# Row maxima of 64-row halves of the array, and key rows interleaved by four, in an attention and expert kernel

## The reference

```python
def _L0_xattn_ref(x, context, w_qkv, w_proj, b_proj):
    B, N, C = x.shape                      # 8, 256, 128
    H, D = 16, 8
    qkv = (x @ w_qkv.T).reshape(B, N, 3, H, D).transpose(2, 0, 3, 1, 4)
    q, k, v = (qkv[0], qkv[1], qkv[2])
    kv = context.reshape(B, N_c, 2, H, D).transpose(2, 0, 3, 1, 4)
    k = jnp.concatenate([kv[0], k], axis=2)
    v = jnp.concatenate([kv[1], v], axis=2)
    attn = jnp.einsum('bhnd,bhmd->bhnm', q * D ** -0.5, k).astype(jnp.float32)
    attn = jax.nn.softmax(attn, axis=-1)
    out = jnp.einsum('bhnm,bhmd->bhnd', attn, v)
    return out.transpose(0, 2, 1, 3).reshape(B, N, C) @ w_proj.T + b_proj

x = x + _L0_xattn_ref(_layernorm(x), ctx_2048, ...)
x = x + _L0_ffn_ref(_layernorm(x), ...)    # experts; the change leaves this part alone
```

## Time and profile before

| | |
|---|---|
| median of 3 runs | 580.87 us (580.58 to 586.15) |
| the profiled execution: its own time | 579.1 us |
| its span, first to last instruction | 577.5 us |
| attention | about 0 to 370 us |
| router and experts | about 370 to 577 us |
| PE busy over the span | 498.9 us (86%) |
| DVE, ACT, POOL busy | 353.9, 292.7, 196.0 us |

### The profile page before, as it was taken

One profiled execution on the slowest core, in us unless ns is written; L12 is line 12 of the kernel. 1 busy time (PEld: TensorE's weight loads), 2 busy tenths in 40 slices (PEclk: granted clock), 3 DMA queues, 4 the chain that ended last, 5 costly groups with the idle time before them and its releaser, 6 DMA issues. The chain is left out here.

```text
span 577.5 us, 10586 instructions
## 1 busy us (share of the span) xinstructions
PE 498.9 (86%) x3467; PEld 322.9 (56%) x3468; DVE 353.9 (61%) x646; ACT 292.7 (51%) x584; POOL 196.0 (34%) x381
## 2 busy tenths in 40 slices
PE   3479999999999999999999998555499999999940
PEld 1346666666666666666565663244447666666630
DVE  7597687777777787777777770368524333333316
ACT  2136667767767677676776767421023333333310
POOL 7151241331422412411400000103317776677630
PEclk9999999999999999999999999865569999999995
DMA  6802434445244344342332300160101111111116
GB/s 168 185 25 72 94 88 108 95 105 134 75 113 121 87 120 104 91 115 64 76 72 58 90 3 2 36 184 0 14 10 43 41 41 38 39 36 43 42 51 189
DMA packets 32078, 44.39 MB, mean 77 GB/s; under 512 B 5484, under 2 KB 20460, under 8 KB 32036
## 3 DMA queue, kind: packets, MB, share of 16 engines
q1 hardware_dynamic: 27076, 36.88, 25.7%
q0 software_dynamic: 2560, 5.25, 3.6%
q10 hardware_dynamic: 2400, 1.70, 1.2%
HBM read 16.58 MB, written 4.72 MB: 37 GB/s over the span
## 5 line engine op out<-in xcount | busy, mean ns | idle before, releaser
L426 DVE TENSOR_REDUCE max_part<-max_ps 128x2 f32<-128x1024 f32 (+1 forms) x192 | 231.3, 1221 | 79.6 <-PE max_ps L519 42.1
L385 ACT ACTIVATE probs<-exp_ps 128x512 f32<-128x512 f32 x384 | 207.4, 591 | 77.5 <-PE exp_ps L541 72.0
L541 PE MATMUL exp_ps<-blocks,keys 128*128 128x512 f32 x384 | 160.9, 421 | 4.5 <-ACT probs L385 2.3
L519 PE MATMUL max_ps<-keys,blocks 128*128 128x512 f32 x256 | 109.9, 436 | 10.1 <-DMA blocks<-masked 7.0
L541 PEld LDWEIGHTS exp_ps<-blocks,keys 128*128 128x128 f32 x384 | 71.7, 187 | 44.8 <-ACT probs L385 18.5
L551 PE MATMUL pv_ps<-probs,value_cols 128*32 128x256 f32 x1536 | 96.3, 383 | 0.0
L986 DVE TENSOR_TENSOR hidden<-up_ps,silu 128x512 f32<-128x512 f32 x40 | 27.7, 692 | 84.4 <-PE up_ps L1076 82.4
L302 POOL CAST maxes<-rowmax 128x8 fp32r<-128x8 f32 x32 | 6.3, 198 | 178.6 <-DVE rowmax L432 178.6
L519 PEld LDWEIGHTS max_ps<-keys,blocks 128*128 128x128 f32 x256 | 48.4, 191 | 30.2 <-DVE max_part L426 19.2
L551 PEld LDWEIGHTS pv_ps<-probs,value_cols 128*32 128x32 f32 x1536 | 43.3, 109 | 39.4 <-issue 17.1
L879 ACT ACTIVATE hiddenT<-at_ps 128x512 f32<-128x512 f32 x40 | 23.9, 597 | 77.2 <-PE at_ps L1093 68.7
(11 more groups left out here) (148 smaller groups left out, 473.4 us busy)
## 6 DMA issues: line engine op xcount, KB each, us to landing
blocks<-masked SPq DMA_DIRECT2D x93, 128.0 KB
keys<-parts SPq DMA_DIRECT2D x96, 96.0 KB
ctx_v_sb<-ctx_v_dram SPq DMA_DIRECT2D x8, 256.0 KB, 2.9
gate<-gateT_dram SPq DMA_DIRECT2D x8, 256.0 KB, 2.8
up<-upT_dram SPq DMA_DIRECT2D x8, 256.0 KB, 2.6
y_in<-pick_outs SPq DMA_DIRECT2D x8, 256.0 KB, 4.9
raw<-ctx_kT_dram SPq DMA_DIRECT2D x7, 256.0 KB, 2.8
h_rows<-h SPq DMA_DIRECT2D x4, 256.0 KB, 4.9
```

Source lines behind the costliest of these rows:

```text
L385: act.activation(probs[par][:, k, 2 * half:2 * half + 2], exp_ps[u % 2][:].rearrange("p (g n) -> p g n", n=N), ACT.Exp).then_inc(exp_done, 1)
L426: vec.reduce_max(out, bank, axis=AX.X).then_inc(max_done, 1)
L519: mm = pe.matmul(max_ps[w % 2][:, half * BANK:(half + 1) * BANK], blocks[:, t, w, half * P:(half + 1) * P], keys[:, t, 0:NC_], start=True, ...
L541: pe.matmul(exp_ps[u % 2][:], keys[:, t, k * P:(k + 1) * P], blocks[:, t, 2 * half:2 * half + 2, :], start=True, stop=True).then_inc(exp_f ...
```

## The change

The rows of `keys` and `blocks` are laid out anew: dimension i of the quad (0 to 31) has its three product rows in partitions 4i, 4i + 1 and 4i + 2. So heads 0 and 1 lie wholly in partitions 0 to 63 and heads 2 and 3 in 64 to 127. Of the free rows 4i + 3, partitions 3 and 35 of `blocks` hold the maximum's two parts. All of `keys` is first set to -1. The DMAs of `spread_rows` and `spread_blocks` write partitions at a step of four.

The maxima are computed with 64 rows of the array at a time: the two halves of a unit are now two heads, one on the lower and one on the upper 64 rows, each into its own bank, and stand behind one another. Units 0 to 3 are one pair (head, tile of queries) for both halves, units 4 and 5 one head by both tiles. The shapes that VectorE reduces keep their sizes. The scores for the exponential stay matmuls on all 128 rows. The order in a group becomes: exponential unit, upper half, lower half, exponential unit.

```diff
+PAIR = G // 2
+TILE = P // 2
+STEP = 4
+MAX_ROW = 3
@@ spread_blocks, spread_rows
-                engine.dma_start(blocks_f[ROWS * j:ROWS * (j + 1), t], masked[ROWS * t:ROWS * (t + 1), c % 2, part])\
+                engine.dma_start(blocks_f[j::STEP, t], masked[ROWS * t:ROWS * (t + 1), c % 2, part])\
-                    sp.dma_start(keys_f[ROWS * j:ROWS * (j + 1), t, :], part[head, 0:KEYS]).then_inc(rows_in[t], 16)
+                    sp.dma_start(keys_f[j::STEP, t, :], part[head, 0:KEYS]).then_inc(rows_in[t], 16)
-                    sp.dma_start(blocks_f[SUM_ROWS:SUM_ROWS + 2, t], blocks_f[SUM_ROWS + 2:SUM_ROWS + 4, t])\
+                    sp.dma_start(blocks_f[MAX_ROW:TILE:ROWS, t], blocks_f[MAX_ROW + STEP:TILE:ROWS, t])\
+            sp.wait_ge(rows_const, 1)
-                    sp.dma_start(blocks_f[SUM_ROWS:SUM_ROWS + 2, q], maxT_f[:, (s + 1) % 2, :]).then_inc(max_in[q], 16)
+                    sp.dma_start(blocks_f[MAX_ROW:TILE:ROWS, q], maxT_f[:, (s + 1) % 2, :]).then_inc(max_in[q], 16)
@@ vector
-            vec.memset(keys[SUM_ROWS:P].bitcast(F32), -1.0).then_inc(rows_const, 1)
+            vec.memset(keys[:].bitcast(F32), -1.0).then_inc(rows_const, 1)
@@ max_half (its third argument is now a, the half of the array)
+                t, rows = q % T, slice(TILE * a, TILE * (a + 1))
...
-                    mm = pe.matmul(max_ps[w % 2][:, half * BANK:(half + 1) * BANK], blocks[:, t, w, half * P:(half + 1) * P],
-                                   keys[:, t, 0:NC_], start=True, stop=True)
+                    g, i = divmod(w, QT)
+                    mm = pe.matmul(max_ps[w % 2][:, a * BANK:(a + 1) * BANK], blocks[rows, t, PAIR * a + g, i * P:(i + 1) * P],
+                                   keys[rows, t, 0:NC_], start=True, stop=True)
...
-                                       blocks[:, t, 2 * (w - G) + half, i * P:(i + 1) * P], keys[:, t, NC_:KEYS],
-                                       start=True, stop=True)
+                        mm = pe.matmul(max_ps[w % 2][:, first:first + N], blocks[rows, t, PAIR * a + w - G, i * P:(i + 1) * P],
+                                       keys[rows, t, NC_:KEYS], start=True, stop=True)
@@ the step on PE
-                    for half in range(2):
-                        if has_scores(s + 2):
-                            max_half(s + 2, i, half)
-                        if has_scores(s):
-                            exp_unit(s, 2 * i + half)
+                    if has_scores(s):
+                        exp_unit(s, 2 * i)
+                    if has_scores(s + 2):
+                        max_half(s + 2, i, 1)
+                        max_half(s + 2, i, 0)
+                    if has_scores(s):
+                        exp_unit(s, 2 * i + 1)
```

More of the change, by code:

```diff
@@ L41 @@
 ROWS = 32
-SUM_ROWS = 3 * ROWS
 SCALE = float(D) ** -0.5
@@ L140, in attend @@
         value_cols = sb("value_cols", [P, T, KT, G, ROWS])
-        max_part, rowmax = sb("max_part", [P, 2, 2, G, QT]), sb("rowmax", [P, 2, G, QT])
+        max_part, rowmax = sb("max_part", [P, 2, 2, 2, PAIR, QT]), sb("rowmax", [P, 2, G, QT])
         maxes, maxT = sb("maxes", [P, 2, QT, P], F32R), sb("maxT", [2 * G, 2, N], F32R)
@@ L382, in step @@
                             wait_for(act, pv_filled, s - 1)
-                        k, half = divmod(u, 2)
+                        k, a = divmod(u, 2)
                         act.wait_ge(exp_filled, s * XUNITS + u + 1)
-                        act.activation(probs[par][:, k, 2 * half:2 * half + 2],
-                                       exp_ps[u % 2][:].rearrange("p (g n) -> p g n", n=N), ACT.Exp).then_inc(exp_done, 1)
+                        act.activation(probs[par][:, k, PAIR * a:PAIR * (a + 1)],
+                                       exp_ps[a][:].rearrange("p (g n) -> p g n", n=N), ACT.Exp).then_inc(exp_done, 1)
                 if r == 0 and b >= 1:
@@ L421, in reduce_unit @@
                 if w < G:
-                    out, bank = max_part[:, par, 0, w, :], max_ps[w % 2][:].rearrange("p (q n) -> p q n", n=NC_)
-                else:
-                    pair = slice(2 * (w - G), 2 * (w - G) + 2)
-                    out, bank = max_part[:, par, 1, pair, :], max_ps[w % 2][:].rearrange("p (g q n) -> p g q n", g=2, n=N)
+                    g, i = divmod(w, QT)
+                    out, bank = max_part[:, par, 0, :, g, i], max_ps[w % 2][:].rearrange("p (a n) -> p a n", n=NC_)
+                else:
+                    out, bank = max_part[:, par, 1, :, w - G], max_ps[w % 2][:].rearrange("p (a q n) -> p a q n", a=2, n=N)
                 vec.reduce_max(out, bank, axis=AX.X).then_inc(max_done, 1)
@@ L431, in row_maxima @@
                 wait_for(vec, split_max, 2 * (q - 1))
-                vec.tensor_tensor(rowmax[:, par], max_part[:, par, 0], max_part[:, par, 1], ALU.max)\
+                merged = max_part[:, par].rearrange("p k a g q -> p k (a g) q")
+                vec.tensor_tensor(rowmax[:, par], merged[:, 0], merged[:, 1], ALU.max)\
                    .then_inc(rowmax_ready, 1)
@@ L510, in project_values, with max_half @@
                 mm.then_inc(v_filled, 1)
-            def max_half(q, w, half):
-                t = q % T
-                if w == 0 and half == 0:
+            def max_half(q, w, a):
+                t, rows = q % T, slice(TILE * a, TILE * (a + 1))
+                if w == 0 and a:
                     pe.wait_ge(rows_in[t], rows_spread(q))
-                if half == 0:
+                if a:
                     wait_for(pe, max_done, q * MUNITS + w - 1)
                 if w < G:
-                    mm = pe.matmul(max_ps[w % 2][:, half * BANK:(half + 1) * BANK], blocks[:, t, w, half * P:(half + 1) * P],
-                                   keys[:, t, 0:NC_], start=True, stop=True)
+                    g, i = divmod(w, QT)
+                    mm = pe.matmul(max_ps[w % 2][:, a * BANK:(a + 1) * BANK], blocks[rows, t, PAIR * a + g, i * P:(i + 1) * P],
+                                   keys[rows, t, 0:NC_], start=True, stop=True)
                 else:
                     for i in range(QT):
-                        first = half * BANK + i * N
-                        mm = pe.matmul(max_ps[w % 2][:, first:first + N],
-                                       blocks[:, t, 2 * (w - G) + half, i * P:(i + 1) * P], keys[:, t, NC_:KEYS],
-                                       start=True, stop=True)
-                if half:
+                        first = a * BANK + i * N
+                        mm = pe.matmul(max_ps[w % 2][:, first:first + N], blocks[rows, t, PAIR * a + w - G, i * P:(i + 1) * P],
+                                       keys[rows, t, NC_:KEYS], start=True, stop=True)
+                if a == 0:
                     mm.then_inc(max_filled, 1)
@@ L536, in exp_unit @@
             def exp_unit(q, u):
-                t, (k, half) = q % T, divmod(u, 2)
+                t, (k, a) = q % T, divmod(u, 2)
                 if u == 0:
@@ L540, in exp_unit @@
                 wait_for(pe, exp_done, q * XUNITS + u - 1)
-                pe.matmul(exp_ps[u % 2][:], keys[:, t, k * P:(k + 1) * P], blocks[:, t, 2 * half:2 * half + 2, :],
-                          start=True, stop=True).then_inc(exp_filled, 1)
+                pe.matmul(exp_ps[a][:], keys[:, t, k * P:(k + 1) * P], blocks[:, t, PAIR * a:PAIR * (a + 1)], start=True, stop=True)\
+                  .then_inc(exp_filled, 1)
             def pv_tile(q, k):
```

## The result

The changed kernel takes 610.01 us (median of 4 runs, 607.88 to 614.61) against 581.39 us for the kernel before (4 runs); the ratio is 1.0485, with a 95% interval from 1.0402 to 1.0568. It is slower by some 29 us; 617 were forecast. The profiled execution has a span of 606.3 us, 28.8 more than before.

What follows compares the result with a forecast made beforehand. PE was taken to set the pace, with about 0.52 us of waits a step. 1.73 us added less 0.52 gave 1.2 us for 30 steps, 36 us: 579.1 + 36 = 615, 617 for the median; range 567 to 632.

Steps and rivals of the forecast that it cites:

- the likeliest case: 64-row form charged like the value batch's 128*32, halves side by side: 595 to 632 us, chance 0.56.
- (2): On PE, each change between 128 and 64 rows: 0.34 us to the next load, 0.10 for the load.
- (1): Two 64-row halves of a maximum unit stream side by side on PE, saving 6 x 0.235 = 1.4 us a step.
- The forecast's lower bound: On PE, both halves start together: 1.085 us a group, 1.185 with 256 columns, 1.07 us more a step.
- (3): The group's new order gives ACT and DVE more time, so all 0.52 us a step of PE's waits go.
- (4, 5): DMAs to every fourth partition and the memset of all of `keys` cost nothing.
- (6): PE's granted clock stays at 1.00; pauses of 0.1 to 0.2 us should not lower it.
- A: Rival: the array's row form changes free of charge on PE, 10 to 15 us faster, about 568 us; chance 0.23.
- B: Rival: PE's load can't be fetched ahead but nothing drains; 0.4 us a step, about 582 us; chance 0.12.
- C: Rival: PE's array drains and the two halves don't overlap, starting 0.235 us apart; some 636 us; chance 0.07.
- D: Rival: the DMA of L221 comes late, 1 us a step, 610 us on top of A; chance 0.02.

Runs made afterwards that it cites:

- halved exponentials: ScalarE's exponentials on 256 of 512 columns, in the changed kernel and the kernel before: 10.80 and 10.05 us a step; whole times don't compare.
- the turned alternation: Kernel before with each group's order turned to exponential unit, maximum half, exponential unit, maximum half: 579.9 us, ratio 0.9985.

## Why the prediction was right, and where it was not

The direction, the mechanism and the size held: 617 forecast, 610 measured, inside the likeliest case's range of 595 to 632. The parts did not all hold. PE's own work was put some 23 us too high and its waits some 13 us too low, and 3 us at the start were not foreseen; together that makes 29 where 36 were forecast. That the sum came out so near is in part luck.

*The price of a change of form* (2) was taken from the value batch: 0.34 us to the next load and 0.10 for the load. Measured: 0.33 and 0.10. Right. The Trainium skill, "TensorEngine Tiling (Array Packing)", Key Properties, has a change of mode drain the engine; for 64 rows the trace now agrees, with 0.24 us of idle time ahead of each maximum load.

*Two halves side by side* (1): right, and better than put. The forecast gave the lower half's load 0.10 us of its own. Both halves lie in one record of 0.49 us, so the second load is hidden. The forecast's lower bound, 1.085 us a group, was the true one (1.10 with halved exponentials), and for units 4 and 5 it is the same 1.10 instead of 1.285. PE's own work grew by 6 x (1.10 - 0.94) = 1.0 us a step, not by 1.73.

*The waits* (3) are the step that failed. The forecast let all 0.52 us a step disappear, because PE now gives its readers more time; with 1.0 us of added work and 0.86 measured, only some 0.1 went. It looked at one buffer at a time: its reader has 0.97 us and comes round after 1.20. But two neighbouring exponential matmuls fill both buffers within 0.4 us, ScalarE reads them one behind the other, 1.09 us for both, and the next but one waits for the second. The rows of the kernel before, 60 to 340 us, to be held against those of the changed kernel above:

```profile
L541 PEld LDWEIGHTS exp_ps<-blocks,keys 128*128 128x128 f32 x324 | 60.7, 187 | 33.0 <-issue 13.0 <-ACT probs L385 11.8
...
L519 PEld LDWEIGHTS max_ps<-keys,blocks 128*128 128x128 f32 x217 | 40.8, 188 | 16.2 <-DVE max_part L426 14.4
```

The waits of these loads for VectorE did go, from 14.4 us to 2.1, as forecast; those for ScalarE grew, from 11.8 to 19.5. In the changed kernel, ScalarE and the load it releases:

```profile
264.41 1.09 ACT L391 ACTIVATE probs<-exp_ps 128x512 f32<-128x512 f32 x2 [0.27 <-PE exp_ps L548]
...
265.54 0.19 PEld L548 LDWEIGHTS exp_ps<-blocks,keys 128*128 128x128 f32 x1 [0.25 <-ACT probs L391]
```

The pair ends at 265.50, the load goes at 265.54 and its matmul 0.10 later; after the matmul before it, whose load began at 265.11, it could have streamed at 265.11 + 0.10 + 0.235 = 265.44. That is the group's 0.20. Maxima on all rows show the order's price by itself, 0.24 us a step; the turned alternation, free of cost, shows that the neighbours are its cause. So a step's 0.86 us are 0.24 for the order and 0.62 for the form on top of it, and not 1.73 less 0.52.

*DMAs and memset* (4, 5): right, 1.0013 (0.9978 to 1.0048) for the layout alone. *The clock* (6): right from 60 to 340 us, where it is granted 1.00, and wrong at the start. The reasoning took the stretch of exponentials on 128 rows as proof that pauses don't matter. In the changed kernel the 1.2 GHz level of the start lasted through the steps with maxima alone and the first one with both kinds, and the first value batch came 3.6 us late.

The sum, then: 30 x 0.24 = 7 for the order, 30 x 0.62 = 19 for the form, 3 at the start, 29 in all.

*The rivals*: A, the form changes free of charge, is ruled out by the pauses; B, only the load open, by their length, 0.33 where a matmul streams 0.235; C, halves one after the other, by the record of 0.49; D, a late DMA, by the layout alone.

## What to carry to other kernels

A part of the array saves streaming only if one stays in that form: here each excursion saved one matmul of 0.235 us and cost two changes of 0.2 us each, and with all score matmuls in the same form the same idea gained 0.75%. Look in the trace for a change of form that is already there; its price carried over within 0.01 us. With two buffers, an in-order queue wants work that waits for another reader between every two matmuls that wait for the same one; when that holds, ask next whether the first matmul after a break starts any later, since on the engine that then decides, each such delay is paid in full at every turn.

## What the runs showed of the hardware that was not expected

The clock fell where the records show PE always busy: with four changes of form a group, matmuls at 0.43 us from one to the next, the granted clock from 60 to 340 us was 0.88 in the profiled execution, in whole stretches 0.50, and the record of a matmul with its open load was 0.79 instead of 0.50 us long. With two changes a group it stayed at 1.00 over the same stretch. What in the pauses does it was not isolated.

At the start, where PE waits for VectorE, all seven kernels with 64-row maxima have the lower level through the first step with both kinds. Of the five with maxima on all rows two (before, and the turned alternation) have nothing of it there, and three have it for a part: with the layout alone, matmuls stand 0.43 us apart from 40.57 to 43.56, where 0.235 is usual.

The clock column may not show it: in the changed kernel it says 1.00 for the first 50 us, while the lengths are those of 1.2 GHz. The lengths of a known matmul were the better witness here.

Matmuls on different rows of the array, even of different kinds (an exponential on the lower, a maximum on the upper half), start within 0.01 us of each other.
